# Moving the quantiser's reads to GpSimd's queue and deferring the softmax scaling in an eight-core attention + FP4 feed-forward kernel

## The chip, the cores and the metric

The kernel runs on the 8 cores of one Trainium2 chip. Each core takes one of the 8 batch elements and works by itself, with no exchange between cores. The metric is the device time of the slowest core in microseconds (us). The engines are called as in the profile: PE (TensorE), PEld (its weight load), DVE (VectorE), ACT (ScalarE), POOL (GpSimd) and SP (SyncE, which here only issues DMAs).

## The reference

For a batch element x of 2048 rows by 1024 columns, the layer normalises each row and adds two branches to x:

```python
xn = _layernorm(x, axis=-1)
x = x + _L0_attn_ref(xn, ...) + _L0_ffn_ref(xn, ...)
# attention: Q, K by a Poincare-ball linear layer (asinh, sinh, a norm per row), V = xn @ w_v.T + b_v
# 16 heads of 64: softmax(Q K^T / 8) V
# feed-forward: every operand is quantised in blocks of 16 to the FP4 grid and back:
scale = max(|block|) / 6;  q = GRID[searchsorted(MID, |x/scale|)] * sign(x/scale) * scale
gate = q(xn) @ q(w_gate).T;  y = q(xn) @ q(w_up).T;  h = silu(gate) * y;  out = q(h) @ q(w_down).T
```

The inner width of the feed-forward is 2816. All data are float32.

## The kernel before

The program is written as a list of operations (`P.op`) with the tiles that each reads and writes. Every engine runs its own operations strictly in the order in which they were written down, and a wait is put ahead of an operation for each tile that it needs. So the written order is also the order of each DMA queue: `P.op(SY, ...)` puts a transfer on SP's queue, `P.op(GP, ...)` on POOL's. Barriers separate the stages.

1. Constants of the two Poincare layers (0 to about 330 us of the trace).
2. Projections (to about 1890 us): four blocks of 512 rows. In each, statistics, the q projection, the k projection and two waves of the v projection; q, k and xn are written to DRAM by POOL's queue (L530, L666).
3. Attention (to about 3970 us): four chunks of 512 queries (`ch`), in each eight pairs of heads (`hp`). `load_pair` loads the next pair's q and k on SP's queue (L712, L717). For a pair, PE computes the scores (L735) into banks of psA, ACT takes the exponential (L745), and PE multiplies by v (L752) into psB. V has a column of ones, so the 65th row of that product is the softmax's sum. ACT copies the product to `at_t` (L760) and the sum to a one-row buffer (L764), and SP's queue moves that row into `rs_t` (L768). At the end of a chunk comes the scaling block: DVE's reciprocal of `rs_t` (L772), then eight times a small PE matmul that spreads it over 128 partitions (L774), DVE's multiplication (L778), and the write of the scaled tile to `at_sp` (L781).
4. Gate and up products with quantisation of h (to about 5322 us), and 5. the down product, with the attention result and x added (to the end).

The quantiser is `emit_qtile` (L305 to L376), called a unit here. It works on one tile of 128 by 512 (some are 128 by 256) and is made of one read from DRAM (L315), nineteen DVE operations (L318 transpose, L320 block maximum, L324, L327, then L333 to L372), and one write to DRAM (L374). L333 is the first operation that writes the buffer `u`, from which the previous unit's write to DRAM is taken, so it waits for that write. L315 may be issued as soon as L318 of the previous unit has read the input buffer. There are 172 such units: 48 stand among the projections (twelve per block, in groups of three), and 124 in the attention stage (`emit_unit`), four ahead of each pair of heads but none ahead of the last pair of a chunk (`hp == 7`); the four that are left over come right behind the scaling block.

On SP's queue a pair of heads therefore reads, in this order: the next pair's q and k loads, four unit reads (L315), and two row moves (L768), whose rows ACT's copy (L764) of the next pair must wait for.

Of the kernel before, what the change touches and what calls it, by code (L numbers as in the profile page):

```python
# [7 lines left out]
A = mybir.AluOpType  # L8
# [9 lines left out]
MT = 8  # L18
# [3 lines left out]
SY, TE, VE, SC, GP = "sync", "tensor", "vector", "scalar", "gpsimd"  # L22
# [119 lines left out]
def build(S=2048):  # L142
# [30 lines left out]
    at_sp = dtmp("at_sp", [D, S])  # L173
# [5 lines left out]
    P = Prog()  # L179
# [37 lines left out]
    psA = nc.alloc_psum_tensor("psA", [128, 2048], F32).ap()  # L217
# [87 lines left out]
    def emit_qtile(src, dst, r0, cs, W, SL=None, NM="nx_", ch="xn0"):  # L305
# [4 lines left out]
        else:  # L310
# [1 line left out]
        K_in, K_t, K_u, K_a, K_g, K_h, K_bm, K_sc = (  # L312
            NM + "in", NM + "t", NM + "u", NM + "a", NM + "g", NM + "h",
            NM + "bm", NM + "sc")
        P.op(SY, lambda e: e.dma_start(  # L315
            out=_in[:, 0:W], in_=src[r0:r0 + 128, cs:cs + W]),
            writes=[K_in], dma=ch)
        P.op(VE, lambda e: e.transpose(_t[:, 0:W], _in[:, 0:W]),  # L318
# [353 lines left out]
    SC2 = 512  # L672
# [28 lines left out]
    def emit_unit():  # L701
        if q_next[0] < len(qunits):
            emit_qtile(*qunits[q_next[0]])
            q_next[0] += 1
            return True
        return False
# [3 lines left out]
    def load_pair(ch, hp):  # L710
# [4 lines left out]
        for pi in range(NVT // KP):  # L715
# [2 lines left out]
                out=K2buf[hp % 2][:, csl], in_=k_sp[hp * 128:(hp + 1) * 128, csl]),  # L718
                writes=[("kb", (hp % 2, pi))], dma=f"k{hp % 2}p{pi}")

    load_pair(0, 0)
    for ch in range(NC2):
        chs = slice(ch * SC2, (ch + 1) * SC2)
        for hp in range(8):
            if hp < 7:
                load_pair(ch, hp + 1)
            elif ch + 1 < NC2:
                load_pair(ch + 1, 0)
            if hp != 7:
                for _ in range(per_iter):  # L730
                    emit_unit()
            for tk in range(NVT):
                for par in range(2):
                    bank = par * 2 + (tk % 2)
                    P.op(TE, lambda e, hp=hp, tk=tk, par=par, bank=bank: e.matmul(  # L735
                        psA[:, bank * 512:(bank + 1) * 512],
                        K2buf[hp % 2][par * 64:(par + 1) * 64,
                                      tk * 128:(tk + 1) * 128],
                        Q2buf[hp % 2][par * 64:(par + 1) * 64, :],
                        start=True, stop=True),  # L740
                        reads=[("kb", (hp % 2, tk // KP)), ("qb", hp % 2)],
                        writes=[("psA", bank)])
                for par in range(2):
                    bank = par * 2 + (tk % 2)
                    P.op(SC, lambda e, tk=tk, par=par, bank=bank: e.activation(  # L745
                        Et[par][tk], psA[:, bank * 512:(bank + 1) * 512],
                        AF.Exp, scale=0.125),
                        reads=[("psA", bank), "consts"],
                        writes=[("eb", (par, tk))])
            for tk in range(NVT):  # L750
                for par in range(2):
                    P.op(TE, lambda e, hp=hp, tk=tk, par=par: e.matmul(  # L752
                        psB[0:65, par * 512:(par + 1) * 512],
                        vt_t[tk][:, (2 * hp + par) * 65:(2 * hp + par) * 65 + 65],
                        Et[par][tk],
                        start=(tk == 0), stop=(tk == NVT - 1)),
                        reads=[("eb", (par, tk)), ("vt", tk)],
                        writes=[("psB", par)])
            for par in range(2):
                P.op(SC, lambda e, hp=hp, par=par: e.activation(  # L760
                    at_t[hp][par * 64:(par + 1) * 64, :],
                    psB[0:64, par * 512:(par + 1) * 512], AF.Copy),
                    reads=[("psB", par)], writes=[("at", hp)])
                P.op(SC, lambda e, par=par: e.activation(  # L764
                    rs_scr[par], psB[64:65, par * 512:(par + 1) * 512],
                    AF.Copy),
                    reads=[("psB", par)], writes=[("rss", par)])
                P.op(SY, lambda e, hp=hp, par=par: e.dma_start(  # L768
                    out=rs_t[2 * hp + par:2 * hp + par + 1, :],
                    in_=rs_scr[par]),  # L770
                    reads=[("rss", par)], writes=["rs"], dma="rs")
        P.op(VE, lambda e: e.reciprocal(rs_t, rs_t), reads=["rs"], writes=["rs"])  # L772
        for mt in range(MT):
            P.op(TE, lambda e, mt=mt: e.matmul(  # L774
                psA[:, 0:512], selb[:, mt * 128:(mt + 1) * 128], rs_t,
                start=True, stop=True),
                reads=["rs", "sel"], writes=[("psA", 0)])
            P.op(VE, lambda e, mt=mt: e.tensor_tensor(  # L778
                at_t[mt], at_t[mt], psA[:, 0:512], A.mult),
                reads=[("at", mt), ("psA", 0)], writes=[("at", mt)])  # L780
            P.op(GP, lambda e, mt=mt, chs=chs: e.dma_start(  # L781
                out=at_sp[mt * 128:(mt + 1) * 128, chs], in_=at_t[mt]),
                reads=[("at", mt)], dma="at")
        for _ in range(per_iter):
            emit_unit()
    while emit_unit():
        pass

# [228 lines left out]
```

How the kernel before makes its waits and increments, by code:

```python
            def body(eng):  # L112
                for waits, fn, sem, inc in self.ops[name]:
                    for s in sorted(waits):
                        v = waits[s]
                        if hwm.get(s, -1) >= v:
                            continue
                        eng.wait_ge(sems[s], v)
                        hwm[s] = v
                    if fn is None:
                        if inc:
                            eng.nop(nofuse=True).then_inc(sems[sem], inc)
                        continue
                    fn(eng).then_inc(sems[sem], inc)
```

## Time and profile before

| | us |
|---|---|
| median of the 2 runs shown | 6325.19 |
| lowest and highest of them | 6108.81 and 6541.58 |
| the profiled execution | 6101.31 |
| its span (core 6, the slowest) | 6099.8 |
| the shortest core's span | 6075.7 |

The two runs are far apart. The profiled execution stands beside the lower one, and all comparisons below are with it. In the profile, "busy" is the time in which an engine executes; a wait is counted on the engine that waits, with the instruction that released it. For a DMA, "us to landing" runs from the issuing instruction's start to the last byte's arrival.

### The profile page before, as it was taken

The numbers are of one execution on the slowest core, as the hardware profiler recorded it, in microseconds if no ns is written. First come the engines' busy times: TensorE is split into PE (matmuls) and PEld (weight loads), VectorE is DVE, ScalarE is ACT, GpSimd is POOL, SyncE is SP. The second block draws the span as 40 slices with busy tenths as digits, with TensorE's granted clock in tenths as the row PEclk, the third lists the DMA queues.
The fourth block names the chain that finished last, engine by engine and source line by source line (L and its number), as shares of the span: only waits on it lengthen the run. The fifth ranks groups of instructions, "written<-read, shape, count | busy, mean of one in ns | idle before, by whom it ended". The sixth has DMA issues, their size and how long they took to land.

```text
span 6099.8 us, 44680 instructions; the slowest of 8 cores (6075.7 to 6099.8 us)
## 1 busy us (share of the span) xinstructions
PE 4552.1 (75%) x10500; PEld 1759.4 (29%) x10500; DVE 3138.3 (51%) x4722; ACT 1036.4 (17%) x1860; POOL 191.5 (3%) x358
## 2 busy tenths in 40 slices
PE   4666565666756876878577587679999999698777
PEld 1112111111112332333233232234444444243333
DVE  0245455446456775775777577427667666600000
ACT  2220220220212332333223132200000000000000
POOL 0000000000000000000000000000000000000000
PEclk9986786877878887888788788889999999898888
DMA  1123122122122221211111121120101101033343
GB/s 53 47 66 93 47 84 96 45 91 78 59 83 78 61 58 45 61 59 47 61 52 59 49 61 51 49 82 28 42 35 35 42 35 35 35 124 119 125 124 115
DMA packets 186594, 397.48 MB, mean 65 GB/s; under 512 B 20833, under 2 KB 68065, under 8 KB 182514
## 3 DMA queue, kind: packets, MB, share of 16 engines
q1 hardware_dynamic: 157138, 286.60, 15.7%
q0 software_dynamic: 29216, 108.03, 4.7%
q8 instruction: 109, 1.79, 0.1%
q14 instruction: 131, 1.07, 0.1%
HBM read 286.41 MB, written 108.00 MB: 65 GB/s over the span
## 4 chain that ended last, share of the span: by engine, by line
PE 47%; DVE 28%; DMA 13%; issue 7%; ACT 2%; DVEq 1%; SPq 0%; POOL 0%; POOLq 0%; ACTq 0%; PEldq 0%
PE psB L822 10%; PE psA L816 10%; PE psB L443 8%; PE psA L928 5%; PE psB L928 5%; DVE b_scr L344 4%; PE psA L622 3%; DMA wqu_d<-b_scr 3%; DMA wqd_d<-b_scr 2%; DMA xq_sp<-b_scr 2%; DMA out_fm<-b_scr 2%; PE psB L752 2%; DMA b_pw<-wv_T 1%; DMA wqg_d<-b_at 1%; DVE b_scr L369 1%
## 5 line engine op out<-in xcount | busy, mean ns | idle before, releaser
L735 PE MATMUL psA<-b_qk 64*128 64x512 f32 x2048 | 602.9, 693 | 502.3 <-ACT b_x L745 443.2
L816 PE MATMUL psA<-b_vt,b_qk 128*128 128x512 f32 x1408 | 724.3, 596 | 71.4 <-DMA b_qk<-wqu_d 39.1
L822 PE MATMUL psB<-b_vt,b_qk 128*128 128x512 f32 x1408 | 722.9, 595 | 23.2 <-DVE b_xn L830 23.2
L443 PE MATMUL psB<-b_xn,b_pw 128*128 128x512 f32 x1024 | 595.3, 671 | 161.3 <-DMA b_pw<-zk_t 57.6
L735 PEld LDWEIGHTS psA<-b_qk 64*128 64x128 f32 x2048 | 333.7, 210 | 773.2 <-issue 767.7
L752 PE MATMUL psB<-b_x,b_vt 128*65 128x512 f32 x832 | 426.5, 594 | 0.0
L928 PE MATMUL psA<-b_vt,b_qk 128*128 128x512 f32 x704 | 332.9, 615 | 92.4 <-DMA b_qk<-wqd_d 56.1
L816 PEld LDWEIGHTS psA<-b_vt,b_qk 128*128 128x128 f32 x1408 | 266.7, 191 | 417.2 <-issue 417.2
L822 PEld LDWEIGHTS psB<-b_vt,b_qk 128*128 128x128 f32 x1408 | 266.9, 191 | 369.1 <-issue 369.1
L928 PE MATMUL psB<-b_vt,b_qk 128*128 128x512 f32 x704 | 330.2, 610 | 56.4 <-DVE b_scr L942 56.4
L622 PE MATMUL psA<-b_pw,b_xn 128*128 128x512 f32 x512 | 276.1, 702 | 106.7 <-DMA b_pw<-wv_T 106.4
L942 DVE SCALAR_TENSOR_TENSOR b_scr<-psA,b_scr 128x512 f32<-128x512 f32 x16 | 11.1, 692 | 649.3 <-DMA b_scr<-at_sp 454.4
L443 PEld LDWEIGHTS psB<-b_xn,b_pw 128*128 128x128 f32 x1024 | 164.7, 199 | 602.4 <-issue 602.4
L745 ACT ACTIVATE b_x<-psA 128x512 f32<-128x512 f32 x416 | 248.7, 598 | 326.0 <-PE psA L735 324.4
L344 DVE SCALAR_TENSOR_TENSOR b_scr<-b_scr 128x512 f32<-128x512 f32 x372 | 251.1, 675 | 39.7 <-DVE b_scr L340 0.9
L830 DVE SCALAR_TENSOR_TENSOR b_xn<-psB,b_xn 128x2048 f32<-128x2048 f32 x22 | 50.4, 2292 | 414.5 <-ACT b_xn L828 414.5
L752 PE MATMUL psB<-b_at,b_vt 128*65 128x512 f32 x512 | 261.4, 592 | 0.0
L333 DVE TENSOR_TENSOR b_scr<-b_scr,b_ct 128x512 f32<-128x512 f32 x124 | 83.7, 675 | 309.6 <-DMA wqu_d<-b_scr 113.5
L457 DVE SCALAR_TENSOR_TENSOR b_scr<-psB,b_sm,b_at 128x512 f32<-128x512 f32 x64 | 47.6, 749 | 333.3 <-PE psB L487 276.5
L928 PEld LDWEIGHTS psA<-b_vt,b_qk 128*128 128x128 f32 x704 | 137.3, 197 | 273.7 <-issue 273.5
L928 PEld LDWEIGHTS psB<-b_vt,b_qk 128*128 128x128 f32 x704 | 135.2, 194 | 237.6 <-issue 237.6
L752 PE MATMUL psB<-b_qk,b_vt 128*65 128x512 f32 x384 | 196.1, 592 | 0.0
(172 smaller groups left out, 4808.3 us busy)
## 6 DMA issues: line engine op xcount, KB each, us to landing
b_qk<-wqd_d SPq DMA_DIRECT2D x88, 512.0 KB, 4.0
b_pw<-wv_T SPq DMA_DIRECT2D x64, 512.0 KB, 3.9
b_qk<-k_sp SPq DMA_DIRECT2D x128, 256.0 KB, 4.8
hq_sp<-b_qk POOLq DMA_DIRECT2D x22, 1024.0 KB, 4.1
b_vt<-hq_sp SPq DMA_DIRECT2D x88, 256.0 KB, 4.2
b_pw<-zq_t SPq DMA_DIRECT2D x40, 512.0 KB, 3.4
b_pw<-zk_t SPq DMA_DIRECT2D x40, 512.0 KB, 3.5
b_scr<-wd_T SPq DMA_DIRECT2D x44, 256.0 KB, 3.3
```

Source lines behind the costliest of these rows:

```text
L333: P.op(VE, lambda e: e.tensor_tensor(_u[:, 0:W].rearrange("p (b c) -> p b c", c=16), _t[:, 0:W].rearrange("p (b c) -> p b c", c=16), rcb, ...
L344: P.op(VE, lambda e, th=th: e.scalar_tensor_tensor(_g[:, 0:W], _a[:, 0:W], th, _g[:, 0:W], A.is_gt, A.add), reads=[K_a, K_g], writes=[K_g])
L369: P.op(VE, lambda e: e.scalar_tensor_tensor(_g[:, 0:W], _a[:, 0:W], 1.0, _t[:, 0:W], A.subtract, A.mult), reads=[K_a, K_t], writes=[K_g])
L443: P.op(TE, lambda e, wb=wb, kt=kt, pv=pv: e.matmul(pv, wb[:, kt * 128:(kt + 1) * 128], xn_t[kt], start=(kt == 0), stop=(kt == KT - 1)), re ...
L622: e.matmul(pvv, xn_t[kt][:, tt * 128:(tt + 1) * 128], wb[:, nh2 * 512:(nh2 + 1) * 512], start=(kt == 0), stop=(kt == KT - 1)),
L735: P.op(TE, lambda e, hp=hp, tk=tk, par=par, bank=bank: e.matmul(psA[:, bank * 512:(bank + 1) * 512], K2buf[hp % 2][par * 64:(par + 1) * 64 ...
L745: P.op(SC, lambda e, tk=tk, par=par, bank=bank: e.activation(Et[par][tk], psA[:, bank * 512:(bank + 1) * 512], AF.Exp, scale=0.125), reads ...
L752: P.op(TE, lambda e, hp=hp, tk=tk, par=par: e.matmul(psB[0:65, par * 512:(par + 1) * 512], vt_t[tk][:, (2 * hp + par) * 65:(2 * hp + par) ...
L816: P.op(TE, lambda e, m=m, kt=kt, n=n: e.matmul(psA[:, n * 512:(n + 1) * 512], wgbuf[m % 2][:, kt * 128:(kt + 1) * 128], xq_t[kt][:, n * 51 ...
L822: P.op(TE, lambda e, m=m, kt=kt, n=n: e.matmul(psB[:, n * 512:(n + 1) * 512], wubuf[m % 2][:, kt * 128:(kt + 1) * 128], xq_t[kt][:, n * 51 ...
L830: P.op(VE, lambda e: e.scalar_tensor_tensor(h_t, psB[:, 0:S], 1.0, sg_t, A.mult, A.mult), reads=[("psB", n) for n in range(NTQ)] + ["sg"], ...
L928: P.op(TE, lambda e, kt=kt, m=m, pp=pp: e.matmul(pp[:, (m % 4) * 512:(m % 4) * 512 + 512], wdbuf[kt % 2][:, m * 128:(m + 1) * 128], hqbuf[kt],
```

## The change

There are four edits in one.

- The unit's read (L315) goes from SP's queue to POOL's queue, where the unit's write (L374) already is.
- The scaling block of a chunk is put into a function, `mk_at_block`, and is emitted in the next chunk's first pair, behind `load_pair` and ahead of the units; that pair then emits eight units instead of four. The last chunk's block is emitted behind the loop.
- Within the block, the small matmul goes to bank 2 of psB instead of bank 0 of psA, and the write to `at_sp` goes from POOL's queue to SP's.
- The row moves (L768) have a key and a semaphore for each of the two heads of a pair instead of a common one.

```diff
-        P.op(SY, lambda e: e.dma_start(
+        P.op(GP, lambda e: e.dma_start(
             out=_in[:, 0:W], in_=src[r0:r0 + 128, cs:cs + W]),
             writes=[K_in], dma=ch)
...
+    def mk_at_block(ch):
+        chs = slice(ch * SC2, (ch + 1) * SC2)
+
+        def blk():
+            P.op(VE, lambda e: e.reciprocal(rs_t, rs_t),
+                 reads=["rs"], writes=["rs"])
+            for mt in range(MT):
+                P.op(TE, lambda e, mt=mt: e.matmul(
+                    psB[:, 1024:1536], selb[:, mt * 128:(mt + 1) * 128], rs_t,
+                    start=True, stop=True),
+                    reads=["rs", "sel"], writes=[("psB", 2)])
+                P.op(VE, lambda e, mt=mt: e.tensor_tensor(
+                    at_t[mt], at_t[mt], psB[:, 1024:1536], A.mult),
+                    reads=[("at", mt), ("psB", 2)], writes=[("at", mt)])
+                P.op(SY, lambda e, mt=mt, chs=chs: e.dma_start(
+                    out=at_sp[mt * 128:(mt + 1) * 128, chs], in_=at_t[mt]),
+                    reads=[("at", mt)], dma="at")
+        return blk
+
+    pending_at = [None]
     load_pair(0, 0)
     for ch in range(NC2):
-        chs = slice(ch * SC2, (ch + 1) * SC2)
         for hp in range(8):
             if hp < 7:
                 load_pair(ch, hp + 1)
             elif ch + 1 < NC2:
                 load_pair(ch + 1, 0)
-            if hp != 7:
-                for _ in range(per_iter):
-                    emit_unit()
+            nq = per_iter if hp != 7 else 0
+            if pending_at[0] is not None:
+                pending_at[0]()
+                pending_at[0] = None
+                nq += per_iter
+            for _ in range(nq):
+                emit_unit()
...
-                    reads=[("rss", par)], writes=["rs"], dma="rs")
-        P.op(VE, lambda e: e.reciprocal(rs_t, rs_t), reads=["rs"], writes=["rs"])
...
-        for _ in range(per_iter):
-            emit_unit()
+                    reads=[("rss", par)], writes=[("rs", par)],
+                    dma=f"rs{par}")
+        pending_at[0] = mk_at_block(ch)
+    pending_at[0]()
+    pending_at[0] = None
```

What this does to the order is shown at three places. First POOL's queue at the start of the attention stage (L374 is the unit's write, L315 its read; `wqu_d` and `wu_T` are the quantised and the raw up-projection weights). Before:

```order
L122 NO_OP [waits s22_scalar,s24_sync,s25_tensor,s26_vector]
L374 DMA wqu_d<-b_scr 128x512 [waits s26_vector] x5
L374 DMA wqu_d<-b_scr 128x256 [waits s26_vector]
L374 DMA wqu_d<-b_scr 128x512 [waits s26_vector] x5
L374 DMA wqu_d<-b_scr 128x256 [waits s26_vector]
```

And after:

```order
L122 NO_OP [waits s23_scalar,s25_sync,s26_tensor,s27_vector]
L315 DMA b_scr<-wu_T 128x512
L374 DMA wqu_d<-b_scr 128x512 [waits s27_vector]
L315 DMA b_scr<-wu_T 128x512 [waits s31_xn0]
L374 DMA wqu_d<-b_scr 128x512 [waits s27_vector]
L315 DMA b_scr<-wu_T 128x512 [waits s31_xn0]
```

Each unit's read now stands behind the previous unit's write, and that write waits for DVE (`vector`), which is to say for the previous unit's last operation.

Second, SP's queue from one pair of heads to the next in the first chunk (L712 and L717 are the q and k loads, L768 the row moves, which are L791 in the changed file). Before:

```order
L315 DMA b_scr<-wu_T 128x512 [waits s26_vector,s30_xn0] x4
L768 DMA b_xn<-b_xn 1x16x32 [waits s21_rs,s22_scalar] x2
L712 DMA b_qk<-q_sp 128x512 [waits s20_q1,s25_tensor]
L717 DMA b_qk<-k_sp 128x512 [waits s13_k1p0]
L717 DMA b_qk<-k_sp 128x512 [waits s14_k1p1]
L717 DMA b_qk<-k_sp 128x512 [waits s15_k1p2]
L717 DMA b_qk<-k_sp 128x512 [waits s16_k1p3]
L315 DMA b_scr<-wu_T 128x512 [waits s26_vector,s30_xn0]
```

After:

```order
L791 DMA b_xn<-b_xn 1x16x32 [waits s21_rs0,s23_scalar]
L791 DMA b_xn<-b_xn 1x16x32 [waits s22_rs1,s23_scalar]
L712 DMA b_qk<-q_sp 128x512 [waits s20_q1,s26_tensor]
L717 DMA b_qk<-k_sp 128x512 [waits s13_k1p0]
L717 DMA b_qk<-k_sp 128x512 [waits s14_k1p1]
L717 DMA b_qk<-k_sp 128x512 [waits s15_k1p2]
L717 DMA b_qk<-k_sp 128x512 [waits s16_k1p3]
```

Nothing on SP's queue waits for DVE any more between two pairs of heads.

Third, PE at the end of the first chunk (L752 is the last product with v, L774 the block's matmul, L735 the next chunk's first scores). Before:

```order
L752 MATMUL psB<-b_xn,b_vt 65x512 [waits s22_scalar,s25_tensor]
L774 MATMUL psA<-b_xn 128x512 [waits s3_cc,s26_vector]
L774 MATMUL psA<-b_xn 128x512 [waits s25_tensor,s26_vector] x7
L735 MATMUL psA<-b_qk 128x512 [waits s9_k0p0,s19_q0,s25_tensor,s26_vector]
L735 MATMUL psA<-b_qk 128x512 x3
```

After (the same operations are L775, L728 and L758):

```order
L775 MATMUL psB<-b_xn,b_vt 65x512 [waits s23_scalar,s26_tensor]
L728 MATMUL psB<-b_xn 128x512 [waits s3_cc,s21_rs0,s22_rs1,s27_vector]
L728 MATMUL psB<-b_xn 128x512 [waits s26_tensor,s27_vector] x7
L758 MATMUL psA<-b_qk 128x512 [waits s9_k0p0,s19_q0]
L758 MATMUL psA<-b_qk 128x512 x3
```

PE's sequence is the same; the next chunk's first scores no longer wait for DVE. DVE's sequence is the same throughout the program, too: the same units and blocks in the same places.

## Rows read from the trace of the kernel before

**Rows 1.** The trace by stage: us, busy time per engine, PE's clock, DMA share.
```profile
330.00:1890.00 1560.00, 955.55 (x1656) 280.28 (x1656) 800.77 (x1343) 258.25 (x436) 77.75 (x144) 0.77 0.23 75
1890.00:3970.00 2080.00, 1549.80 (x4160) 629.03 (x4160) 1363.72 (x2392) 606.48 (x1152) 84.45 (x156) 0.85 0.19 57
```
**Rows 2.** Waits of the whole execution: engine, line, releaser; us in total, times, longest.
```profile
PE psA L735 <- ACT b_x L745: 443.2, 28, 47.0
ACT b_xn L764 <- DMA b_xn<-b_xn: 430.1, 31, 46.3
DVE b_vt L636 <- PE psA L622: 128.7, 20, 27.0
DVE b_xn L772 <- DMA b_xn<-b_xn: 104.8, 4, 27.3
```
**Rows 3.** The unit's write (L374): who waited for it, us and times.
```profile
  DVE b_scr L333: 309.2, 120
  DVE b_at L333: 68.0, 32
```
**Rows 4.** Waits of SP's own queue: the largest.
```profile
SPq L118 <- DVE b_scr L318: 1552.1, 119, 28.5
```
**Rows 5.** DVE in order of time, from one unit to the next.
```profile
2216.16 0.71 DVE L372 STREAM_TRANSPOSE b_scr<-b_scr 128x512 f32<-128x512 f32 x1
2216.79 0.67 DVE L318 STREAM_TRANSPOSE b_scr<-b_scr 128x512 f32<-128x512 f32 x1
...
2221.91 0.69 DVE L333 TENSOR_TENSOR b_scr<-b_scr,b_ct 128x512 f32<-128x512 f32 x1 [2.92 <-DMA wqu_d<-b_scr]
```
**Rows 6.** POOL in order of time: that unit's write, and eight writes in a row.
```profile
2217.40 0.54 POOL L374 DMA_DIRECT2D wqu_d<-b_scr  x1 [14.57 <-DVE b_scr L372]
...
798.64 4.72 POOL L530 DMA_DIRECT2D q_sp<-b_qk  x8 [6.07 <-DVE b_qk L526]
```
**Rows 7.** DMA issues of the attention stage: KB each, median us to landing.
```profile
b_scr<-wd_T SPq DMA_DIRECT2D x44, 256.0 KB, 3.3
wqd_d<-b_scr POOLq DMA_DIRECT2D x44, 256.0 KB, 4.0
at_sp<-b_at POOLq DMA_DIRECT2D x32, 256.0 KB, 2.6
b_qk<-k_sp SPq DMA_DIRECT2D x128, 256.0 KB, 4.8
```
**Rows 8.** Single issues: at 2217.40, 2302.97, 2327.86, and the second of eight at 799.
```profile
wqu_d<-b_scr POOLq DMA_DIRECT2D x1, 256.0 KB, 4.3
...
wqu_d<-b_scr POOLq DMA_DIRECT2D x1, 256.0 KB, 2.3
...
b_scr<-wu_T SPq DMA_DIRECT2D x1, 256.0 KB, 2.7
...
q_sp<-b_qk POOLq DMA_DIRECT2D x1, 256.0 KB, 3.5
```
**Rows 9.** DVE at the first chunk's end.
```profile
2328.99 3.34 DVE L772 RECIPROCAL b_xn<-b_xn 16x512 f32<-16x512 f32 x1 [26.56 <-DMA b_xn<-b_xn]
...
2356.09 0.70 DVE L318 STREAM_TRANSPOSE b_scr<-b_scr 128x512 f32<-128x512 f32 x1
...
2358.43 0.69 DVE L333 TENSOR_TENSOR b_scr<-b_scr,b_ct 128x512 f32<-128x512 f32 x1
```
**Rows 10.** The chain that ended last, last pair of the first chunk: start, us, what.
```profile
2280.16 16.50 PE psA L735 x46
2296.66 26.77 PE psB L752 x62
```
**Rows 11.** First unit read of the attention stage on SP, and its DVE user.
```profile
1896.64 0.59 SPq L315 DMA_DIRECT2D b_scr<-wu_T  x1
...
1903.07 0.71 DVE L318 STREAM_TRANSPOSE b_scr<-b_scr 128x512 f32<-128x512 f32 x1 [23.97 <-ACT b_x L745]
```
**Rows 12.** PE in the second projection block, the reciprocal behind three units.
```profile
922.47 2.04 PE L522 MATMUL psB<-b_at,b_sm 1*128 1x512 f32 x2 [13.74 <-DVE b_at L521]
```

More of the change, by code:

```diff
@@ L770, in build @@
                     in_=rs_scr[par]),
-                    reads=[("rss", par)], writes=["rs"], dma="rs")
-        P.op(VE, lambda e: e.reciprocal(rs_t, rs_t), reads=["rs"], writes=["rs"])
[L773 to L783, printed above, removed]
-        for _ in range(per_iter):
-            emit_unit()
+                    reads=[("rss", par)], writes=[("rs", par)],
[3 more added lines that the diff above has]
+    pending_at[0] = None
     while emit_unit():
```

## The prediction

> **What bounds the kernel now.** I read the table by stage first, to see which engine is busy in the two stages that the change touches [rows 1]. In the attention stage (1890 to 3970 us) PE is busy for 1549.8 of 2080 us and DVE for 1363.7, so the shares alone don't name the bound. The waits do. PE waits 443 us for ACT's exponential, and ACT waits 430 us for the one-row move into `rs_t` [rows 2]. DVE waits in two places: 309.2 us in 120 times at L333 for the previous unit's write [rows 3], and 104.8 us in 4 times at L772 [rows 2]. A chain is visible. The row moves stand on SP's queue behind four unit reads, and that queue waited 1552 us for DVE's L318 [rows 4]. So DVE is the clock of the stage: its units hold back SP's reads, these hold back the row moves, and the row moves hold back ACT and PE. DVE's own account closes: 1363.7 busy, 309.2, 104.8, and the rest in gaps between its instructions and ahead of the block's multiplications. The stage is as long as DVE's chain.
>
> From one unit's write to the next it is 14.57 + 0.54 = 15.1 us [rows 6]. From the end of L372 (2216.87) to the start of L333 of the next unit (2221.91) it is 5.04 us, of which 2.92 are idle, so 2.12 us are the unit's head, L318 to L327 [rows 5]. The mean idle time is 309.2 / 120 = 2.58 us, hence on average 2.12 + 2.58 = 4.70 us from L372's end to L333.
>
> In the projections PE waits up to 13.74 us at L522 for DVE's reciprocal, which stands behind three units [rows 12]. The DVE chain ends last there as well.
>
> **The read on POOL's queue.** This is the edit that decides. Before, the next unit's read is issued as soon as L318 has read the buffer, well over 10 us before it is wanted; it is hidden wholly. After, it stands behind the write, which waits for L372. So the step from one unit to the next is a chain:
> - L372's end to the write's issue: 2217.40 - 2216.87 = 0.53 us [rows 5, 6].
> - The write occupies POOL: eight in a row take 4.72 us, 0.59 each [rows 6].
> - The read from issue to landing: L, unknown, below.
> - Landing to the operation that waits: a write issued at 2217.40 landed 4.3 later, at 2221.7, and L333 began at 2221.91 [rows 5, 6, 8]; with the rounding I take 0.15.
> - L318 to L333 with nothing in the way: 2358.43 - 2356.09 = 2.34 us [rows 9].
>
> That is 3.61 + L, against 4.70 before: each exposed unit grows by L - 1.09 us. The write's landing no longer matters, since it was issued before the read and L333 comes 2.34 us after the read is in. Behind DVE's new wait stand all of the unit's operations, then the next units and the scaling block; PE waits for the block, and POOL for the next write.
>
> No row shows a DRAM read from POOL's queue, so L is bounded. From below: a write of 256 KB on POOL with no read in flight landed in 2.3 us, and a lone read on SP in 2.7 [rows 8]; the block's writes took a median 2.6 [rows 7]. From above: the k loads, four or five at once, took 4.8, and the unit's write, which crosses a read in flight, 4.0 [rows 7]. Nearer by: the same reads on SP, which cross a write, took 3.3 [rows 7], and the second of a row of POOL writes 3.5 [rows 8]. After the change the read comes 0.59 us behind one write, and no other unit transfer is in flight. I take L = 3.0, between the lone read and the crossed one: each exposed unit grows by 1.9 us.
>
> The Trainium skill (DMA: Bandwidth & Descriptors, "Anatomy of one DMA — SWDGE (gpsimd) path") fits a DMA from GpSimd as 2.0 us plus its bytes over 436 GB/s, 2.6 us for 256 KB. The block's writes here, median 2.6 [rows 7], agree; by that rule L would be 2.6 and the sum below 109 us instead of 165.
>
> In the attention stage 120 of 124 units are exposed; the first of each chunk's run is read during the block or at the start. 120 x 1.9 = +228 us.
>
> In the projections the mean wait is 68.0 / 32 = 2.13 us [rows 3], so a unit grows by 1.9 + 0.45 = 2.35. A group has three units, whose first read is issued early, behind the last group's write, so two are exposed. Of the four groups per block, three stand on the DVE chain (behind q, behind k, behind v's second wave). The one between the two v waves is followed by a wait of DVE for PE, part of the 128.7 us of L636 [rows 2], which hides its growth. So 2 x 3 x 4 = 24 exposures, +56 us. PE's second v wave gains a little, for its weight loads no longer stand behind unit reads; I estimate 7 us over four blocks, since the longer group eats most of it. Together +49.
>
> **SP's queue freed.** Row moves and loads now follow PE and ACT. PE's and ACT's waits of 443 and 430 us [rows 2] become one long wait of PE for the scaling block, for the block's reciprocal stands behind the units on DVE. The stage gains only where DVE waited for PE: at L772, 104.8 us. A pair takes PE 16.5 + 26.8 = 43.3 us [rows 10], with ACT's copies some 46; eight take 368 us. DVE needs 32 x 15.1 = 483 us per chunk before, and some 60 more after. So PE is through with the last pair long before DVE, and the whole 104.8 goes: -105 us. What is late next is DVE itself. Were PE slower by the 170 us between, the wait would be back.
>
> The first unit starts earlier: its read stood behind ten q and k loads, was issued at 1896.64 and used at 1903.07 [rows 11]. On an idle POOL queue it goes out at about 1891. I take -7.
>
> **The deferred block.** PE's and DVE's sequences are unchanged, as the order shows: the block still stands behind hp 7's products and ahead of the next scores on PE, and behind the same units on DVE. It costs the same 27.1 us (2328.99 to 2356.09) [rows 9]. The other bank spares the next scores one multiplication, 0.7 us on PE, which has slack: 0. The block's writes on SP: SP has slack there, 0; last chunk, ahead of the barrier, the same latency. Split keys for the row moves save ACT a move's latency per pair, with slack: 0.
>
> **The sum.** 228 + 49 - 105 - 7 = +165 us on the profiled execution's 6101.3: 6266, written 6270. That execution stands by the lower of the two runs shown (6108.8), not by their median of 6325.2, which lies halfway to 6541.6; the forecast is for an execution of the first sort.
>
> **The rivals.**
> 1. *The read lands as fast as an undisturbed transfer.* L between 2.3 and 2.67. At 2.3 a unit grows by 1.21: 120 x 1.21 = 145, 24 x 1.66 - 7 = 33, less 112: +66, 6168. At 2.6: 181 + 40 - 112 = +109, 6210. For it: the 2.3 and 2.6 us of POOL's writes and the 2.7 us of the lone read [rows 7, 8]. Against it: a write is always just ahead, and k loads come by. By the Trainium skill's fit (same page and section) this is the case to expect.
> 2. *The read is as slow as a crossed transfer.* At L = 4.0: 120 x 2.91 = 349, 24 x 3.36 - 7 = 74, less 112: +311, 6412. At 4.8: 445 + 93 - 112 = +426, 6527. For it: the 4.0 us of writes that cross a read, on this very queue [rows 7]. Against it: they cross on two queues, which is over.
> 3. *Faster: POOL issues the read ahead of the write's wait.* If the read left before L372's end, it would be hidden as before, L333 would wait 2.58 us as before, and only the gains were left: 105 + 7 + 7 = 119, 5982. It decides from the point where a read is issued more than 3 us before the write. Against it stands the order: the write waits for DVE, and the read is behind it on one queue.
> 4. *The change does nothing.* The deferral alone does nothing by the order; but the queue move is real.
>
> **How the numbers follow.** A measurement of this kernel can tell about 2%, 122 us, from no change. My sum passes that from L = 2.7 up. Forecast (L from 2.7 to 4.0): 0.60. Rival 1: 0.29, within 2%. Rival 2: 0.07. Rival 3: 0.03, and it is just on the edge of 2%. Rest, 0.01, within 2%. So slower 0.67, same 0.30, faster 0.03. The range goes from rival 1 at L = 2.3 to somewhat beyond rival 2's lower end: 6165 to 6450.
>
> **What would show it right or wrong.** Right: DVE's waits at L333 near 0, and a new wait at L318 for the read, about 120 times in the attention stage, 1.27 + L + some 0.1 = 4.3 us each, some 520 us in all; L772's counterpart (L725) no longer waits; ACT's wait for row moves near 0; PE waits once per chunk, over 100 us, for DVE's reciprocal. The attention stage grows by about 116 us and the projections by about 50; the later stages stay. Wrong: a wait at L318 below 3.5 us (rival 1) or above 5.2 (rival 2); reads issued before the write (rival 3); or a wait at L725, which would mean that PE didn't get ahead.

## The result and the profile after

The changed kernel is slower: the ratio to the kernel before is 1.046, with a 95% interval of 1.041 to 1.051, some 280 us. The forecast was a ratio of 1.027 (+165 us). So the direction and the mechanism came as predicted, and the size was some 40% short. In some executions of every kernel here, the profiled one of the changed kernel among them, one die or both run at a lower clock and take up to 9% longer; the ratios and the forecast are for the others. These took 6368.9 to 6401.6 us with the change, inside the forecast's range of 6165 to 6450 (over all executions the medians are 6763.9 us after and 6516.1 before). So of the changed kernel's profile only DVE's waits are read below; lengths of stages are read from experiment 2, the kernel before with the reads on POOL's queue and nothing else.

First DVE's new wait. Two views of the changed kernel follow (core 1): the line of the read with those who waited for it (us, times), and the list of waits (engine, line, releaser; us in total, times, longest).

```profile
L315 POOL DMA_DIRECT2D b_scr<-wu_T x48: 541/541/543, 1972.2 to 2810.7; - x48
...
who waited for it (us, times):
  DVE b_scr L318: 621.4, 121
  DVE b_at L318: 156.2, 36
...
DMA to landing us min/median/max: 2.7/3.5/9.1
```

```profile
PE psB L728 <- DVE b_xn L725: 483.6, 4, 156.8
...
DVE b_scr L318 <- DMA b_scr<-wu_T: 253.7, 47, 18.3
DVE b_scr L318 <- DMA b_scr<-wd_T: 202.6, 43, 7.3
DVE b_scr L318 <- DMA b_scr<-xn_sp: 165.2, 31, 8.8
...
PE psB L522 <- DVE b_at L521: 142.1, 4, 38.0
```

The 309.2 us at L333 [rows 3] are gone, and L318, which had waited only at the start, waits 621.4 us in 121 times, 5.14 each where I had expected 4.3. One of the 121 is the stage's first unit, 18.3 us; the other 120 are 5.03 each. No transfer is waited for at L333 or at the chunk's reciprocal (L725) any more; PE now waits for that reciprocal, once per chunk. ACT's wait for the row moves, 430.1 us [rows 2], has shrunk to 1.6.

The chain by which the read came to be exposed stands in POOL's order of time (start, us, engine, line, tiles; in brackets the idle time before) and in DVE's, core 6, beside [rows 5, 6]:

```profile
2235.57 0.54 POOL L374 DMA_DIRECT2D wqu_d<-b_scr  x1 [16.87 <-DVE b_scr L372]
2236.11 0.54 POOL L315 DMA_DIRECT2D b_scr<-wu_T  x1
2248.03 0.54 POOL L374 DMA_DIRECT2D wqu_d<-b_scr  x1 [11.38 <-DVE b_scr L372]
2248.56 0.54 POOL L315 DMA_DIRECT2D b_scr<-wu_T  x1
```

```profile
2247.05 0.45 DVE L372 STREAM_TRANSPOSE b_scr<-b_scr 128x256 f32<-128x256 f32 x1
2251.52 0.71 DVE L318 STREAM_TRANSPOSE b_scr<-b_scr 128x512 f32<-128x512 f32 x1 [4.03 <-DMA b_scr<-wu_T]
```

L372 ends at 2247.50, the write goes out 0.53 us later, the read 0.53 behind it (I had put 0.59), and L318 starts 2.96 us after that. This is one of the quicker reads: its wait is 4.03 us. In the DMA issues of the changed kernel (KB each, median us to landing) the attention stage's reads of the weights take within 0.1 us what they took on SP's queue (`wd_T` 3.3 [rows 7]), those of `xn_sp` 0.4 more, and the writes take less:

```profile
b_scr<-wd_T POOLq DMA_DIRECT2D x44, 256.0 KB, 3.4
wqd_d<-b_scr POOLq DMA_DIRECT2D x44, 256.0 KB, 2.4
...
b_scr<-wu_T POOLq DMA_DIRECT2D x40, 256.0 KB, 3.4
...
b_scr<-xn_sp POOLq DMA_DIRECT2D x32, 256.0 KB, 3.8
```

Before, on SP's queue:

```profile
b_scr<-xn_sp SPq DMA_DIRECT2D x32, 256.0 KB, 3.4
```

Where the time stands: the stages of experiment 2's kernel, core 3 (stretch; its length; busy time of PE, PEld, DVE, ACT and POOL; PE's clock, DMA share, GB/s). The cuts between stages are the attention stage's first load and the first gate product.

```profile
330.00:1954.30 1624.30, 912.86 (x1660) 267.29 (x1658) 809.46 (x1350) 259.54 (x439) 102.43 (x191) 0.78 0.23 72
1954.30:4261.80 2307.50, 1528.15 (x4160) 607.94 (x4160) 1377.77 (x2392) 608.48 (x1152) 150.25 (x280) 0.81 0.17 54
4261.80:6391.20 2129.40, 1859.74 (x4224) 805.72 (x4224) 915.04 (x878) 89.10 (x67) 28.97 (x54) 0.94 0.21 66
```

The kernel before, cut in the same places (core 6; the columns are the same):

```profile
330.00:1890.80 1560.80, 955.55 (x1656) 280.28 (x1656) 800.77 (x1343) 258.25 (x436) 77.75 (x144) 0.77 0.23 75
1890.80:3991.50 2100.70, 1549.80 (x4160) 629.03 (x4160) 1363.72 (x2392) 606.48 (x1152) 84.45 (x156) 0.84 0.20 59
3991.50:6099.80 2108.30, 1859.52 (x4224) 806.09 (x4224) 915.01 (x878) 89.11 (x67) 29.07 (x54) 0.94 0.21 66
```

The attention stage grew by 206.8 us (forecast 116), the projections by 63.5 (forecast 49), and the last stages by 21.1 (forecast 0); together 291.4, the whole difference of the two spans.

### The profile page after: what moved, and what is told of

The parts are those of the page before. It is cut to its first block, busy times and chain, and to the rows that moved or that the text cites. A ratio compares the mean times of both kernels' runs of the same rounds, so it can differ in the third digit from the quotient of the medians.

```text
span 6771.5 us, 44544 instructions; the slowest of 8 cores (6487.3 to 6771.5 us)
## 1 busy us (share of the span) xinstructions
PE 5135.0 (76%) x10500; PEld 1929.2 (28%) x10500; DVE 3156.3 (47%) x4722; ACT 1057.9 (16%) x1860; POOL 265.2 (4%) x498
## 4 chain that ended last, share of the span: by engine, by line
PE 44%; DVE 32%; DMA 12%; issue 8%; ACT 2%; POOL 1%; DVEq 1%; SPq 0%; POOLq 0%; ACTq 0%; PEldq 0%
PE psB L835 11%; PE psA L829 11%; PE psB L443 7%; PE psA L941 5%; PE psB L941 5%; DVE b_scr L344 4%; DMA b_scr<-wu_T 3%; DMA b_scr<-wd_T 2%; DMA b_scr<-xn_sp 2%; DMA b_at<-wg_T 2%; DVE b_ct L320 2%; DMA out_fm<-b_scr 2%; DVE b_at L344 1%; PE psA L622 1%; DVE b_scr L318 1%
## 5 line engine op out<-in xcount | busy, mean ns | idle before, releaser
L829 PE MATMUL psA<-b_vt,b_qk 128*128 128x512 f32 x1408 | 858.0, 696 | 65.6 <-DMA b_qk<-wqu_d 37.2
L835 PE MATMUL psB<-b_vt,b_qk 128*128 128x512 f32 x1408 | 858.2, 696 | 19.0 <-DVE b_xn L843 19.0
L758 PE MATMUL psA<-b_qk 64*128 64x512 f32 x2048 | 609.3, 728 | 82.6 <-DVE b_scr L318 80.6
L775 PE MATMUL psB<-b_x,b_vt 128*65 128x512 f32 x832 | 510.8, 701 | 0.0
L941 PE MATMUL psA<-b_vt,b_qk 128*128 128x512 f32 x704 | 397.8, 716 | 96.8 <-DMA b_qk<-wqd_d 57.6
L728 PE MATMUL psB<-b_xn 16*128 16x512 f32 x64 | 65.3, 1120 | 510.3 <-DVE b_xn L725 483.6
L829 PEld LDWEIGHTS psA<-b_vt,b_qk 128*128 128x128 f32 x1408 | 309.5, 221 | 496.7 <-issue 496.7
L941 PE MATMUL psB<-b_vt,b_qk 128*128 128x512 f32 x704 | 396.4, 714 | 56.2 <-DVE b_scr L955 56.2
L758 PEld LDWEIGHTS psA<-b_qk 64*128 64x128 f32 x2048 | 335.7, 215 | 357.6 <-issue 333.9
L835 PEld LDWEIGHTS psB<-b_vt,b_qk 128*128 128x128 f32 x1408 | 309.5, 221 | 449.2 <-issue 449.2
L318 DVE STREAM_TRANSPOSE b_scr<-b_scr 128x512 f32<-128x512 f32 x124 | 86.1, 694 | 621.4 <-DMA b_scr<-wu_T 253.7
L768 ACT ACTIVATE b_x<-psA 128x512 f32<-128x512 f32 x416 | 248.6, 598 | 616.4 <-PE psA L758 602.5
L775 PE MATMUL psB<-b_at,b_vt 128*65 128x512 f32 x512 | 313.3, 699 | 0.0
L941 PEld LDWEIGHTS psA<-b_vt,b_qk 128*128 128x128 f32 x704 | 158.9, 227 | 320.5 <-issue 320.5
L941 PEld LDWEIGHTS psB<-b_vt,b_qk 128*128 128x128 f32 x704 | 157.3, 226 | 280.5 <-issue 280.5
L775 PE MATMUL psB<-b_qk,b_vt 128*65 128x512 f32 x384 | 235.0, 699 | 0.0
```

The lines of the kernel that those rows point to most:

```text
L318: P.op(VE, lambda e: e.transpose(_t[:, 0:W], _in[:, 0:W]), reads=[K_in], writes=[K_t])
L728: P.op(TE, lambda e, mt=mt: e.matmul(psB[:, 1024:1536], selb[:, mt * 128:(mt + 1) * 128], rs_t, start=True, stop=True), reads=["rs", "sel" ...
L768: P.op(SC, lambda e, tk=tk, par=par, bank=bank: e.activation(Et[par][tk], psA[:, bank * 512:(bank + 1) * 512], AF.Exp, scale=0.125), reads ...
L775: P.op(TE, lambda e, hp=hp, tk=tk, par=par: e.matmul(psB[0:65, par * 512:(par + 1) * 512], vt_t[tk][:, (2 * hp + par) * 65:(2 * hp + par) ...
L829: P.op(TE, lambda e, m=m, kt=kt, n=n: e.matmul(psA[:, n * 512:(n + 1) * 512], wgbuf[m % 2][:, kt * 128:(kt + 1) * 128], xq_t[kt][:, n * 51 ...
L835: P.op(TE, lambda e, m=m, kt=kt, n=n: e.matmul(psB[:, n * 512:(n + 1) * 512], wubuf[m % 2][:, kt * 128:(kt + 1) * 128], xq_t[kt][:, n * 51 ...
```

## The experiments

Twelve kernels ran. The quoted text under each edit was written before its run. Ratios are to the kernel before, with 95% intervals.

### 1 and 2. The queue move alone, and all but it

Experiment 1 is the changed kernel with one word put back:

```diff
-        P.op(GP, lambda e: e.dma_start(   # L315
+        P.op(SY, lambda e: e.dma_start(
```

> The changed kernel with one edit undone: the units' reads are on SP's queue again; deferred block, its bank, its writes on SP and the split keys stay. My theory (the read exposed behind the write on POOL's queue is the whole loss, and the rest of the change does nothing): a ratio to the kernel before of 1.00, within 0.5%; DVE waits about 300 us at L333 and about 105 us at the block's reciprocal, as before. Rival (the deferred block or its writes on SP's queue cost something of their own): over 1.01.

Experiment 2 is the kernel before with the opposite edit:

```diff
-        P.op(SY, lambda e: e.dma_start(   # L315
+        P.op(GP, lambda e: e.dma_start(
```

> The kernel before with only the units' reads moved to POOL's queue. My theory: the same ratio as the whole change, 1.046 within 0.7%; some 620 us of waits at L318 in the attention stage, no wait at L772. Rival (the deferral hides part of the loss, or adds to it): it lies over 1% away from 1.046.

Experiment 2 gave 1.050 [1.046, 1.053], as much as the whole change. Experiment 1 gave 0.984 [0.982, 0.986]: the rest of the change isn't neutral, it gains 1.6%. That was a miss. Its profile has no wait at L725, and SP's order of time (core 0) shows why:

```profile
2264.03 0.33 SPq L315 DMA_DIRECT2D b_scr<-wu_T  x1
2264.51 1.16 SPq L791 DMA_DIRECT2D b_xn<-b_xn  x2
...
2268.91 1.73 SPq L791 DMA_DIRECT2D b_xn<-b_xn  x2
```

The same queue in the kernel before:

```profile
2259.20 15.49 SPq L315 DMA_DIRECT2D b_scr<-wu_T  x2
2274.84 5.03 SPq L768 DMA_DIRECT2D b_xn<-b_xn  x2
...
2324.79 2.92 SPq L768 DMA_DIRECT2D b_xn<-b_xn  x2
```

The row moves of the last two pairs of the chunk go out 4.4 us apart now, and went out 50 us apart before, the last ones 4 us ahead of the reciprocal (2328.99 [rows 9]). ACT and PE have gained a pair. The next two runs ask which edit did it.

### 3 and 4. Split keys alone, deferral alone

Theory A for the miss: with a common semaphore ACT's copy of a pair's second head waits for the row move of its first head as well, which stands on SP's queue behind this pair's four reads. Experiment 3 is the kernel before with only this:

```diff
-                    reads=[("rss", par)], writes=["rs"], dma="rs")
+                    reads=[("rss", par)], writes=[("rs", par)],
+                    dma=f"rs{par}")
```

> The kernel before with one edit: the row moves have a key and a semaphore for each of the two heads of a pair. Theory A (with the common semaphore ACT's copy of a pair's second head waits for the row move of its first head, which stands behind this pair's reads on SP's queue; with two semaphores PE and ACT get one pair ahead, so that the last pair of a chunk is done when DVE is): the same as the changed kernel with its reads back on SP, 0.984 within 0.4%, no wait at L772. Rival B (the deferral of the block made that gain): 1.00.

Experiment 4 is experiment 1 with that edit undone, so the deferral alone:

```diff
-                    reads=[("rss", par)], writes=[("rs", par)],
-                    dma=f"rs{par}")
+                    reads=[("rss", par)], writes=["rs"], dma="rs")
```

> The changed kernel with the reads back on SP's queue and the row moves' common key and semaphore back: what is left is the deferred block, its bank and its writes on SP. Theory A (the split keys made the 1.6%): 1.00 within 0.4%, with about 105 us of wait at the block's reciprocal. Rival B (the deferral made it): 0.984.

Neither has a ratio with an interval. The spans of cores 0 to 3 in their profiles are set beside those of cores 0 to 3 of the kernel before, 6079.9 to 6095.9. With split keys alone:

```profile
core 0: 5971.2 us, clock 0.878
core 1: 5964.3 us, clock 0.878
core 2: 5962.3 us, clock 0.878
core 3: 5972.8 us, clock 0.876
```

With the deferral alone they are 6077.0 to 6094.8, the same as before; one whole execution took 6113.4 us, where two of the kernel before beside it took 6090.8 and 6111.5. The waits say it too. The split alone (core 0): the reciprocal never waits, and ACT's wait has halved from 430.1 us:

```profile
ACT b_xn L764 <- DMA b_xn<-b_xn: 208.6, 22, 13.2
```

The deferral alone (the reciprocal's line, core 2) has the wait of [rows 2] unchanged:

```profile
L725 DVE RECIPROCAL b_xn<-b_xn x4: 3341/3341/3341, 2305.6 to 3913.3; 16x512 f32<-16x512 f32 x4
its engine sat idle before it (us, times) until:
  DMA b_xn<-b_xn: 107.6, 4
```

Theory A stands: the split keys are worth some 2% as long as the reads are on SP's queue, and the deferral nothing. Keys and semaphores were split together, so which of the two does it isn't shown.

### 5 and 6. Where the read stands in POOL's queue

Experiment 5 keeps the reads on POOL's queue but puts the next unit's read ahead of this unit's write, so that it waits for L318 only:

```diff
+        if nunit is not None:
+            nsrc, _, nr0, ncs, nW = nunit
+            P.op(GP, lambda e: e.dma_start(
+                out=_in[:, 0:nW], in_=nsrc[nr0:nr0 + 128, ncs:ncs + nW]),
+                reads=[], writes=[K_in], dma=ch)
         P.op(GP, lambda e: e.dma_start(
             out=dst[r0:r0 + 128, cs:cs + W], in_=_u[:, 0:W]),
```

> The changed kernel, but on POOL's queue the read of the next unit stands ahead of the write of this one, so that it waits for L318 and not for L372. My theory: the wait at the unit's transpose goes; the write no longer crosses a read, so it lands in 2.4 us instead of 4.0, and the wait for it falls from 2.58 to about 1.0 us; with the 105 us of the reciprocal gone and the earlier start, the attention stage falls by 120 x 1.6 + 105 + 7 = about 300 us and the projections by some 30, ratio to before 0.945. Rival (transfers on POOL's queue are slow or starved as such, whatever their order): still over 1.02.

Experiment 6 has the same order, but the read is also made to wait for L372, as the write does:

```diff
-                reads=[], writes=[K_in], dma=ch)
+                reads=[K_u], writes=[K_in], dma=ch)
```

> The changed kernel with the next unit's read ahead of this unit's write on POOL's queue, but made to wait for L372 all the same. My theory (a read is exposed for its own latency, and the write ahead of it costs only its time on POOL, 0.54 us): the wait at the unit's transpose shrinks by 0.54 us in 144 exposed units, 78 us, ratio 1.034. Rival (the write ahead also holds up the read's transfer): another 0.5 us or so in each, ratio 1.02 or less.

Experiment 5 gave 0.959 [0.954, 0.963], against an expected 0.945. The wait for the read is gone but for the first one, and the write's wait is back, smaller (core 0; who waited for the write, and the DMA issues):

```profile
  DVE b_scr L335: 204.2, 120
  DVE b_at L335: 44.4, 32
```

```profile
b_scr<-wd_T POOLq DMA_DIRECT2D x44, 256.0 KB, 3.3
wqd_d<-b_scr POOLq DMA_DIRECT2D x44, 256.0 KB, 2.3
...
b_scr<-xn_sp POOLq DMA_DIRECT2D x32, 256.0 KB, 3.6
```

The 1.70 us per wait were expected to be 1.0. In DVE's order of time the median of the 120 waits is 1.04, and the largest tenth is above 3.8: the expectation was right for the typical transfer and missed the tail. The reads take 3.3 and 3.6 us here too. POOL's order of time shows what still goes out just ahead of them:

```profile
2263.61 0.55 POOL L381 DMA_DIRECT2D wqu_d<-b_scr  x1 [9.21 <-DVE b_scr L374]
2264.26 0.54 POOL L378 DMA_DIRECT2D b_scr<-wu_T  x1
```

The read is that of the unit after the next. It goes out 0.65 us behind a write, as in the changed kernel (0.53), but a whole unit earlier than it is wanted. So a write and a read are as close together as before, and what has changed is only that nobody waits for the read.

Experiment 6 gave 1.028 [1.023, 1.032], between the 1.034 of my theory and the 1.02 of its rival. The read is late, but 0.54 us less late (core 0; what L320, the unit's transpose here, waited for, and the DMA issues):

```profile
  DMA b_scr<-wu_T: 205.0, 47
  DMA b_scr<-wd_T: 184.2, 43
  DMA b_scr<-xn_sp: 145.6, 31
```

```profile
b_scr<-wd_T POOLq DMA_DIRECT2D x44, 256.0 KB, 3.5
wqd_d<-b_scr POOLq DMA_DIRECT2D x44, 256.0 KB, 3.6
```

That is 534.8 / 121 = 4.42 us. Without the first unit's wait it is 4.30, where experiment 2, with the write in front, has 4.90 (core 3): the write's 0.54 us on POOL, and little more. With no write just ahead the reads of `wd_T` still take 3.5 us, so their 3.3 isn't a price of the write. Most of the loss is the wait for L372, which the read doesn't need; the write's own slot is the smaller part.

### 7 and 8. A second buffer `u`, in either kernel

If L333's wait for the write is the clock of the kernel before, a second output buffer removes it; after the change it should do nothing. The same edit in both:

```diff
+        if uflip[0] % 2:
+            _u = b_ct[:, 128:640]
+            K_u = NM + "u2"
+        wsem = f"w{uflip[0] % 2}"
+        uflip[0] += 1
...
-            reads=[K_u], dma="sp")
+            reads=[K_u], dma=wsem)
```

> The changed kernel with two buffers u in turn (and a semaphore each), so that no unit waits for the previous unit's write; the read stays behind the write on POOL's queue. My theory (the write's landing no longer matters after the change): nothing, within 0.5% of 1.046. Rival (the write still takes part in the wait): faster than the changed kernel by 1% or more.

> The kernel before with two buffers u in turn (and a semaphore each). If the unit's wait for the write is on the chain of the attention stage, as I read it, its 309 us go there and some 40 of 68 in the projections, ratio 0.943; the wait at L772 stays near 105. Rival (PE and SP's queue are as late as DVE, so that another wait takes its place): over 0.97.

The changed kernel gave 1.051 [1.048, 1.054], no effect: 631.9 us of waits for reads in the attention stage. The kernel before gave 0.956 [0.948, 0.963], against an expected 0.943. The wait for the write is gone, and the attention stage of the profiled execution is 1842.2 us long where it was 2100.7, 258.5 less for a wait of 309.2. Part of the rest is the reciprocal's wait for the row moves, 120 to 131 us on the eight cores where it was 105 to 112 (core 0):

```profile
  DMA b_xn<-b_xn: 130.7, 4
```

So DVE's chain did set the attention stage before, and after the change the write's landing is out of it. What took back the other 30 us or so was not looked into.

### 9. How the loss is shared by the stages

The changed kernel with the reads of the projections on SP's queue:

```diff
-        P.op(GP, lambda e: e.dma_start(
+        P.op(SY if NM == "pq_" else GP, lambda e: e.dma_start(
```

> The changed kernel with the reads of the projections' 48 units back on SP's queue; those of the attention stage stay on POOL's. My theory: the projections are again as long as before (63 us shorter than with the reads moved), the attention stage stays some 207 us longer; ratio 1.036. Rival (both stages hang together by the clock or by the queue): it stays above 1.042.

It gave 1.033 [1.025, 1.040], against an expected 1.036. L318 waits as before in the attention stage (613.7 us in 121 times), and the projections have their old wait at L333 back (72.9 us in 32 times). So the projections hold about 1.3 of the 4.6%.

### 10. Is the tail of the reads made by the loads of q and k?

The loads of q and k are the largest traffic on SP's queue beside the reads. This kernel leaves them out from the third pair of the first chunk on, so its scores are computed from the first two pairs' q and k (the text below says three):

```diff
     def load_pair(ch, hp):
+        if ch > 0 or hp > 1:
+            return
```

> The changed kernel without the q and k loads of the pairs, except the first three pairs' worth at the start (the scores are then computed from stale heads; the exponential, the product and the rest run as before). It asks why the wait at the unit's transpose is 5.1 us on average where the reads' median landing of 3.4 gives 4.6. Theory A (the tail comes from the pairs' loads, which share the DMA engines with the reads): the mean falls to about 4.6 us, some 60 us in all, ratio about 1.037. Rival B (the tail comes from elsewhere, such as the other cores' traffic or the layout of the rows): the mean stays above 4.9, ratio 1.045 or more.

It gave 1.043 [1.032, 1.053], an interval that holds 1.037 as well as 1.045. The waits must decide. The reads of the attention stage still cost DVE 597.5 us in 121 times, 4.94 each (core 3):

```profile
  DMA b_scr<-wu_T: 234.2, 47
  DMA b_scr<-wd_T: 201.7, 43
  DMA b_scr<-xn_sp: 161.6, 31
```

But 18.7 us of them are the first unit's, whose read goes out beside the ten loads that are left. Without it DVE's order of time gives 4.83 us on this core and 4.71 over the eight cores (4.64 to 4.83). Experiment 9, whose attention stage is that of the changed kernel, has 4.93 (4.87 to 4.98) when read the same way. The medians are alike, 4.55 in the mean of the cores, so what fell is the tail: of some 960 waits 28 are above 6 us, where 106 were. So the loads of q and k make more than half of what the mean has above the median (0.17 us left of 0.38), and theory A is nearer than rival B. Where the loads run, it can be seen directly: on core 2 of experiment 9 the 23 waits for a read that was on its way within 6 us of the issue of a q or k load are 6.3 us in the mean, the other 97 are 4.6. What makes the rest of the tail stays open: traffic of other cores and the layout of the rows in DRAM were not tried. In time this is little, some 26 us in 120 waits, which the ratio can't show.

### 11 and 12. What the parts give when put together

Experiment 11 is the kernel before, reads on SP's queue, with the split keys, the second buffer, and the scaling block spread over four banks:

```diff
-                psA[:, 0:512], selb[:, mt * 128:(mt + 1) * 128], rs_t,
+                psA[:, mt % 4 * 512:mt % 4 * 512 + 512],
+                selb[:, mt * 128:(mt + 1) * 128], rs_t,
...
-                reads=["rs", "sel"], writes=[("psA", 0)])
+                reads=["rs", "sel"], writes=[("psA", mt % 4)])
```

> A version meant to win, from the kernel before: split keys for the row moves, two buffers u with a semaphore each, and the scaling block's matmuls over four banks of psA in turn; the reads stay on SP's queue. My theory (DVE's chain is the attention stage): two u alone gave 0.956, the wait of 131 us at the reciprocal goes with the split keys, and the block falls from 27 to some 19 us, 32 us in four; ratio 0.930. Rival (at this pace PE, at 46 us a pair against 50 for four units, takes over): 0.945.

Experiment 12 is the changed kernel with the read ahead of the write, the second buffer, and the block over two banks of psB:

```diff
-                    psB[:, 1024:1536], selb[:, mt * 128:(mt + 1) * 128], rs_t,
+                    psB[:, 1024 + mt % 2 * 512:1536 + mt % 2 * 512],
+                    selb[:, mt * 128:(mt + 1) * 128], rs_t,
...
-                    reads=["rs", "sel"], writes=[("psB", 2)])
+                    reads=["rs", "sel"], writes=[("psB", 2 + mt % 2)])
```

> The changed kernel with the read ahead of the previous unit's write on POOL's queue, two buffers u, and the scaling block over two banks of psB. My theory: no wait is left at the transpose or at L333; against the read-ahead kernel (0.959) another 204 us go in the attention stage, some 30 in the projections and 30 in the blocks; ratio 0.917. Rival (PE becomes the bound of the attention stage): no better than 0.935.

They gave 0.930 [0.920, 0.939] and 0.925 [0.916, 0.935]. Both beat the kernel before and the changed one, and can't be told apart. The reads may stand on either queue, if the write that waits for the end of the unit just before theirs is not ahead of them. DVE hardly waits for a transfer in the attention stage of experiment 12 (core 6, the unit's transpose L326; beside it one reciprocal waits 24.0 us):

```profile
  DMA b_scr<-wu_T: 16.9, 1
```

## Why the prediction was right, and where its size failed

**The mechanism held at each step.** The read waits behind the write for L372 (POOL's order of time; experiments 2, 5 and 6). L333's wait goes, and the write's landing no longer matters (experiment 7). The stage is as long as DVE's chain (experiment 8). The reciprocal never waits, and PE waits for it. The first unit came earlier: L318's wait at the start is 16.0 us in experiment 2, where it was 24.0, -8 for a forecast of -7. The deferral costs and gains nothing (experiment 4).

**The step that failed is L = 3.0.** For the attention stage the ledger closes with DVE's idle times of experiment 2 and of the kernel before: ahead of L318 and L333 together 631.5 for 333.6, so +297.9; at the reciprocal 0 for 104.8; L318 itself busy 86.1 for 81.0, +5.1. The sum is +198.2 of the measured 206.8. Three of experiment 2's 124 waits, 14.8 us in all, stand right behind a scaling block, where this kernel has the block's writes on POOL's queue ahead of the read; the changed kernel has 121 waits and not these. For the other 120 units the way from L372's end to L333's start took 7.21 us in the mean, and 4.67 before: they grew by 2.54 us each and not by 1.9. By the prediction's own formula L was 1.09 + 2.54 = 3.63 on average. The error has two halves. In DVE's order of time the median wait of experiment 2 is 4.56 us; less 0.53, 0.54 and 0.15 that is 3.34, the 3.3 us that the same reads took on SP's queue [rows 7]. I had taken a value between this and one lone read of 2.7 [rows 8], on the ground that no other unit transfer would be in flight beside it; but the reads of the attention stage take 3.2 to 3.8 wherever they stand (experiments 5 and 6), so the row for the same transfer was the one to trust. That is 0.3 us. The other half is mean against median. The mean wait without the start's is 602 / 123 = 4.90, and 19 of these waits are above 5.5 us. More than half of this part goes with the loads of q and k (experiment 10), which the prediction knew as traffic but gave no price. A chain with no slack pays every slow transfer in full. While the read was hidden its tail cost nothing, so the 2.58 us of before, whose median is 2.62, gave no sign of it.

The fit of the Trainium skill (DMA: Bandwidth & Descriptors, "Anatomy of one DMA — SWDGE (gpsimd) path"), 2.6 us for 256 KB, doesn't hold for these reads: 3.4 to 3.8 us in the median. The writes, at 2.4, lie a little below it. Rival 1, which rested on it beside, is out.

**The -105 us were right in size, but the reason was too narrow.** I credited them to SP's queue being free of unit reads. Experiment 2 has them by that alone, experiment 3 by the split keys alone. Either is enough, and together they don't add. "Split keys: 0" was right only because the other edit had already taken the gain; for the kernel before it was wrong by some 2% (experiment 3). Had the change kept the reads on SP's queue, it would have gained 1.6% (experiment 1).

**The projections** grew by 63.5 us (49 forecast): L318 waits 158.3 us in 36 times in experiment 2, 4.40 each, for 68.0 at L333. The forecast had two exposed reads in each of 16 groups, 32 in all. The reads there (`wg_T`) took 3.8 us in the median and not 3.0, so the error is of the same kind; how much of it was covered was not measured. The last 21.1 us stand in the last stages, where 17 of them are longer waits of PE for DVE at the down product. No step of the prediction had them, and no run looked into them.

**The rivals.** Rival 1 is out by the waits of 5 us, rival 3 by POOL's order of time, rival 4 by the result. Rival 2, the slow read, was nearer than I thought: the mean of 3.63 lies past the middle between my 3.0 and its lower end at 4.0.

## What to carry to other kernels

When a transfer changes its queue, look at what stands ahead of it there and what that waits for. A prefetch behind a store that waits for the end of the computation is no prefetch; ahead of the store it is hidden again, on either queue. Price a transfer that becomes exposed by the row of that same transfer, wherever it was issued, and by its mean with the tail, since a chain without slack pays the mean. A key and a semaphore shared by two heads' row moves make a copy wait for a move that it doesn't need; through a queue that was held up elsewhere this cost some 2% here.

## What the runs showed of the hardware

The unit's write of 256 KB on POOL's queue landed in 4.0 us with the next read in flight on SP's queue [rows 7], in 3.6 right behind a read on its own queue (experiment 6), and in 2.3 to 2.4 with a read right behind it (the changed kernel and experiment 5). The order on the queue alone was worth up to 1.3 us. The reads of `wd_T` in the attention stage don't mirror this: 3.3 to 3.5 us in experiments 2, 5 and 6 and the changed kernel. Those of `wg_T` in the projections do in part: 3.8 us in experiment 2 and 4.0 in the changed kernel, 3.2 in experiments 5 and 6, and 3.1 on SP's queue before; why isn't shown. Nor had I expected that the unit reads have so long a tail, 2.7 to 9.1 us for a median of 3.5 in the changed kernel, or that the q and k loads on the other queue make most of it (experiment 10).
